# Attention steps written out for all quads, with constant waits, in place of a loop of four steps

## The chip, the cores and the metric

The kernel runs on one core of a Trainium2 chip. The metric is the device time of one execution in microseconds. The engines are TensorE (PE; its weight loads are listed apart as PEld), VectorE (DVE), ScalarE (ACT), GpSimd (POOL) and SyncE (SP, which here only issues DMAs). Each engine runs its own list of instructions in order; the engines meet through semaphores, on which an instruction can wait and which a finished instruction raises.

## The reference

The input x is 16 batches of 512 tokens of 128 channels. One transformer block is computed in f32, cut here to what matters:

```python
h = layernorm(x)
q, k, v = (h @ w_lat @ w_heads for the three)        # 16 heads of 8
att = softmax(causal(q @ k.T / sqrt(8)))
x = x + layernorm((att @ v) @ w_proj + b_proj)
ys = geglu(x @ Ws1 + bs1) @ Ws2 + bs2                # shared feed-forward
top_val, top_idx = top_k((x @ Wr + br) / 1.5, 2)     # 2 of 12 experts
yr = sum over the two of softmax(top_val) * (geglu(x @ We1[e] + be1[e]) @ We2[e] + be2[e])
x = x + layernorm(ys + yr)
```

## The kernel before, in words

Attention comes first, and it is tiled into 64 **quads**: a quad is four heads of one batch, so four quads make a batch. Steps run from `FIRST` = -2 to `LAST` = 65; step g works on three quads at once. It takes the query-major scores of quad g + 2 (`scores_by_query`, `L1229`), from which VectorE reduces the maximum of every row (`L1664`), in five units of two PSUM banks each; it takes the key-major scores of quad g (`scores_by_key`, `L1261`), also in five units, of which ScalarE makes exponentials (`L948`) and GpSimd masks the diagonal blocks (`L721`); and it multiplies the probabilities of quad g - 1 with the values (`products`, `L1308`). Three pairs of PSUM banks are handed round between these units in a fixed order (`EVEN_ITEMS` and `ODD_ITEMS`, `RING` = 3); `wait_emptied` makes TensorE wait until the former unit of a pair of banks has been read.

The row maxima reach the key-major scores by a detour. VectorE joins and negates them (`L1673`), GpSimd splits them into three bf16 parts (`split_maxima`, `L733` to `L739`), TensorE turns them (`turn_maxima`, `L1276`), ScalarE copies them to SBUF (`copy_max_rows`, `L968`), and SyncE moves them by two DMAs per quad into rows of the query matrix (`L555`), so that the subtraction of the maximum is part of the matmul. The first key-major scores of a quad (unit 1) wait for these DMAs (`s_m`, in `scores_by_key`).

Beside that, SyncE stores the parts of later batches' queries and keys (`L510`), loads the queries and keys of quad g + 3 (`load_quad`, `L503`) and, from quad 56 on, writes blank rows (`L536`). Every second step TensorE turns a finished pair of outputs back (`turn_back`, `L1288`), and VectorE normalises it.

The order within a step is written by hand, per engine (`step`, one function per engine). `quad_steps` runs it: steps -2 to 3 are written out, then a hardware loop (`Fori`) of 13 iterations with four steps each covers quads 4 to 55, and steps 56 to 65 are written out again. In the loop the quad's number is a register's value, so that semaphore counts and DMA addresses are computed from it by the engine. Each engine has a loop of its own.

`wait_apart` is a helper for some of the waits: it issues a wait as an instruction by itself, which also raises a semaphore `passed` that nobody waits for. It is used in the attention steps (`L71`), and in the stages behind them: the shared feed-forward, which scatters the rows by expert (`L833`), and the expert tiles of 128 or 256 rows. Of the expert tiles the first 8 and those from 56 on are written out, and 48 run in a loop of eight tiles. In an expert tile VectorE works out the weights (`routed_as`, `L1967` to `L1974`), adds the bias to the finished product (`L2009`) and multiplies with the weight (`L2011`).

The step numbers that a function gets are `gs`, an integer from which buffers are chosen, and `g`, the quad's number, an integer where the step is written out and a register's value in the loop.

Of the kernel before, what the change touches and what calls it, by code (L numbers as in the profile page):

```python
# [13 lines left out]
B, T, C = 16, 512, 128  # L14
# [53 lines left out]
def wait_apart(engine, sem, value, passed):  # L68

    engine.wait_ge(sem, value)  # L70
    engine.sem_inc(passed, 1)  # L71


def ge(engine, sem, value):
# [5 lines left out]
FIRST, LAST = -2, QUADS + 1  # L80
# [13 lines left out]
EARLY = 2  # L94
# [86 lines left out]
def build(nc, a, out):  # L181
    with ExitStack() as ctx:
# [204 lines left out]

            return ROUTE_STEPS * (n - ns % 2) // 2 + ROUTE_STEPS

        def quad_steps(engine, step):  # L390

            for g in range(FIRST, 4):
                step(g, g)
            with engine.Fori(1, B - EARLY) as it:
                for q in range(4):
                    step(4 + q, 4 * it + q)
            for g in range(4 * (B - EARLY), LAST + 1):
                step(g, g)

        LOOPED = PAIRED // 8  # L400
# [37 lines left out]


        GROUPS = tuple(last for _, last in X_LOADS)  # L440

        def rows_of_batch_ready(engine, b):
# [32 lines left out]
        def _(sp):  # L475
# [55 lines left out]
            def step(gs, g):  # L531
# [8 lines left out]
                if 0 <= gs and gs + 3 < QUADS:  # L540

                    if gs > 0:
                        wait_apart(sp, s_st, UNITS * g, s_passed)
                    if gs == 1:
                        sp.wait_ge(s_first_st[1], sum(PARTS))
                    elif gs % 4 == 1:
                        for s in range(2):
                            for n in range(3):
                                wait_apart(sp, s_parts[s][n], SIDE_PARTS[s][n] // 4 * (g - 1), s_passed)
                    load_quad((gs + 3) % 4, g + 3)  # L550
# [7 lines left out]
                if q and projects(gs - gs % 2):  # L558
                    heads_at = 4 * (g - q) + EARLY * HEADS
                    if q == 1:  # L560
                        wait_apart(sp, s_p1, g - q + 2, s_passed)
                        store_late(heads_at, 0, 0)
                    elif q == 2:
                        wait_apart(sp, s_split, 3 * (g - q) + 6, s_passed)
                        store_late(heads_at, 0, 1)
                        store_late(heads_at, 0, 2)
                    else:
                        wait_apart(sp, s_p1, g - q + 4, s_passed)
                        store_late(heads_at, 1, 0)
                elif q == 0 and projects(gs - 4):  # L570
                    wait_apart(sp, s_split, 3 * g, s_passed)
                    store_late(4 * g + (EARLY - 1) * HEADS, 1, 1)
                    store_late(4 * g + (EARLY - 1) * HEADS, 1, 2)

            quad_steps(sp, step)


            sp.wait_ge(s_st, 5 * QUADS)
# [71 lines left out]
        def _(pool):  # L650
# [148 lines left out]
            def step(gs, g):  # L799
# [10 lines left out]
                else:  # L810
# [8 lines left out]
                    mask_unit(gs, g, 3)  # L819
                    split_rows(gs, g, 2)  # L820

            quad_steps(pool, step)


            def scatter(ns, n):
# [37 lines left out]
        def _(act):  # L863
# [141 lines left out]
            def copy_yT(ns, n):  # L1005
# [2 lines left out]
                ge(act, s_proj, n - 1)  # L1008
                act.activation(yT[:, ns % 2, :], ps[:, YT_TURN, :], ACT.Copy).then_inc(s_yTsb, 1)

            quad_steps(act, step)

            act.wait_ge(s_w2, 160)
            act.wait_ge(s_vcur, QUADS)
# [103 lines left out]
        def _(pe):  # L1118
# [306 lines left out]
                                     start=False, stop=(t == NT - 1))  # L1425
                last.then_inc(s_proj, 1)

            quad_steps(pe, step)

            pe.wait_ge(s_exp, UNITS * QUADS)  # L1430
            pe.transpose(ps[:, BE_TURN, 0:6 * E], be_rows[:], ident[0:6 * E, 0:6 * E]).then_inc(s_beT, 1)
# [133 lines left out]
        def _(dve):  # L1565
# [381 lines left out]
                if ns == TABLE_AT:  # L1947
                    tile_table()

            quad_steps(dve, step)  # L1950

            dve.wait_ge(s_vcur, QUADS)
            dve.memset(counted, 0.0).then_inc(s_cset, 1)
# [118 lines left out]
```

## Time and profile before

| | |
|---|---|
| time, median of 3 runs | 1133.36 us (1133.0 to 1135.47) |
| the profiled execution | 1131.17 us |
| its span | 1129.3 us |
| mean granted TensorE clock | 0.953 |
| TensorE matmuls busy | 992.2 us, 8685 instructions |
| VectorE busy | 853.1 us |
| ScalarE busy | 722.5 us |
| GpSimd busy | 632.7 us |

The times in the trace count from the start of the span. Attention's quad 4 starts at 102.45, quad 56 at 486.94; the scatters run from about 590 to 751; the expert tiles end at about 1067, and the last normalisation follows. Engine overlap makes the busy times add up to far more than the span.

### The profile page before, as it was taken

To read this page: it belongs to the slowest core of one execution; us is meant where nothing else is said; L and a number is where in the kernel's file an instruction comes from. 1 tells how busy PE (TensorE), PEld (TensorE's weight loads), DVE (VectorE), ACT (ScalarE), POOL (GpSimd) and SP (SyncE) were. 2 spreads that over 40 slices of the span, in tenths; PEclk is the share of its full clock that TensorE was granted. 3 is DMA by queue.
4 is the path that set the end of the run, shared out by engine and by line. 5 is a ranking of instruction groups with operands and counts; after the bars stand their busy time and mean duration, and the time that the engine had idled before them with its cause. 6 is when DMAs were issued, how large, how long until landed. Compare 5 with 4: busy or idle time off the path is not lost. (4 is left out here: it accounts for less than half of the span.)

```text
span 1129.3 us, 31995 instructions
## 1 busy us (share of the span) xinstructions
PE 992.2 (88%) x8685; PEld 618.6 (55%) x8685; DVE 853.1 (76%) x2487; ACT 722.5 (64%) x1234; POOL 632.7 (56%) x1195
## 2 busy tenths in 40 slices
PE   4589999999999999978879998759999999998774
PEld 2553344443444434433456665339999888897532
DVE  5678888888888888877689985327777777777646
ACT  4578788888888888866646665316565555556426
POOL 4327777777777777755217777742444444444344
PEclk9889999999999999999959998969999999999988
DMA  8413333333333333343251111122222222221176
GB/s 221 104 31 104 112 104 109 113 106 106 105 107 113 113 110 104 107 115 103 74 214 57 54 54 56 51 80 60 61 66 67 60 65 67 63 61 57 32 252 197
DMA packets 135726, 108.21 MB, mean 96 GB/s; under 512 B 32207, under 2 KB 127866, under 8 KB 135658
## 3 DMA queue, kind: packets, MB, share of 16 engines
q1 hardware_dynamic: 124842, 88.19, 27.8%
q0 software_dynamic: 8544, 17.78, 4.4%
q10 hardware_dynamic: 2272, 1.45, 0.5%
q8 instruction: 28, 0.46, 0.2%
q14 instruction: 40, 0.33, 0.1%
HBM read 56.70 MB, written 50.68 MB: 95 GB/s over the span
## 5 line engine op out<-in xcount | busy, mean ns | idle before, releaser
L1664 DVE TENSOR_REDUCE maxima<-ps 128x8 f32<-128x1024 f32 x320 | 380.4, 1222 | 76.7 <-PE ps L1229 69.8
L948 ACT ACTIVATE pT_area<-ps 128x1024 f32<-128x1024 f32 x320 | 320.8, 1023 | 86.2 <-PE ps L1261 80.9
L843 POOL DMA_INDIRECT ys_dram<-quad_area,place_cur x139 | 133.1, 958 | 188.2 <-issue 126.5
L721 POOL TENSOR_SCALAR_AFFINE_SELECT pT_area<-pT_area 128x256 f32<-128x256 f32 (+1 forms) x448 | 186.6, 439 | 90.8 <-ACT pT_area L948 88.3
L1308 PE MATMUL ps<-pT_area,quad_area 128*32 128x512 f32 (+3 forms) x2048 | 185.5, 446 | 0.6 <-POOL pT_area L721 0.6
L833 POOL DMA_INDIRECT xs_dram<-quad_area,idx_cur x128 | 123.1, 961 | 74.6 <-issue 73.7
L1261 PE MATMUL ps<-quad_area 64*128 64x256 bf16 (+3 forms) x1024 | 125.9, 301 | 30.7 <-DMA quad_area<-mT_sb 28.1
L1991 DVE SCALAR_TENSOR_TENSOR quad_area<-ps,be_cur,xnT 128x256 f32<-128x256 f32 (+1 forms) x228 | 92.0, 456 | 61.5 <-PE ps L1541 28.0
L1530 PE MATMUL ps<-quad_area 128*128 128x256 f32 (+1 forms) x456 | 130.3, 368 | 7.0 <-DVE quad_area L1991 6.8
L1096 ACT ACTIVATE xnT<-ps,be_cur 128x256 f32<-128x256 f32 (+1 forms) x228 | 103.1, 453 | 49.2 <-PE ps L1531 48.1
L1229 PE MATMUL ps<-quad_area 61*128 61x128 bf16 (+2 forms) x1792 | 127.0, 241 | 4.7 <-ACT pT_area L948 2.7
L1531 PE MATMUL ps<-quad_area 128*128 128x256 f32 (+1 forms) x456 | 128.0, 362 | 0.0
L1541 PE MATMUL ps<-outT_area,quad_area 128*128 128x128 f32 x834 | 107.8, 278 | 2.7 <-DVE quad_area L2009 2.3
L1541 PEld LDWEIGHTS ps<-outT_area,quad_area 128*128 128x128 f32 x834 | 102.4, 192 | 10.8 <-issue 5.5
L1229 PEld LDWEIGHTS ps<-quad_area 61*128 61x128 bf16 x1792 | 70.1, 94 | 68.8 <-ACT pT_area L948 50.2
L1261 PEld LDWEIGHTS ps<-quad_area 64*128 64x128 bf16 x1024 | 38.4, 94 | 104.9 <-DVE maxima L1664 65.9
L1531 PEld LDWEIGHTS ps<-quad_area 128*128 128x128 f32 x456 | 84.2, 191 | 10.0
L1530 PEld LDWEIGHTS ps<-quad_area 128*128 128x128 f32 x456 | 78.5, 191 | 17.5 <-DVE quad_area L1991 11.0
L1085 ACT ACTIVATE quad_area<-ps 128x256 f32<-128x256 f32 (+1 forms) x76 | 27.7, 365 | 80.3 <-PE ps L1516 80.3
L1308 PEld LDWEIGHTS ps<-pT_area,quad_area 128*32 128x32 f32 x2048 | 43.7, 108 | 57.8 <-issue 48.0
L1081 ACT ACTIVATE quad_area<-pT_area 128x768 f32 x76 | 63.4, 835 | 0.1
L1238 PE MATMUL ps<-mask_of,mask_to 64*128 64x256 bf16 x512 | 50.8, 273 | 5.9 <-DVE maxima L1664 4.8
(234 smaller groups left out, 1501.9 us busy)
## 6 DMA issues: line engine op xcount, KB each, us to landing
qk_dram<-split_area SPq DMA_DIRECT2D x192, 128.0 KB, 2.3
quad_area<-qk_dram SPq DMA_DIRECT2D x256, 96.0 KB, 2.3
row_area<-xs_dram SPq DMA_DIRECT2D x63, 132.0 KB, 2.1
pT_area<-ys_dram SPq DMA_DIRECT2D x16, 512.0 KB, 5.0
pT_area<-in_L_ffn_We SPq DMA_DIRECT2D x12, 384.0 KB, 6.3
out_dram<-pT_area SPq DMA_DIRECT2D x7, 512.0 KB, 3.0
xs_dram<-row_area SPq DMA_DIRECT2D x5, 528.0 KB, 4.4
split_area<-in_L_ffn_We SPq DMA_DIRECT2D x12, 192.0 KB, 3.8
```

What stands on the lines that cost most here:

```text
L721: return pool.affine_select(out=blocks, in_=blocks, compare_op=ALU.is_ge, fill=0.0, base=0, pattern=[[0, count], [1, P]], channel_multipli ...
L833: pool.indirect_dma_start(xs_dram, at, rows_cur[:, b % DEPTH, t, :], None).then_inc(s_scat[par], 16)
L843: pool.indirect_dma_start(ys_dram, at, ys[:, ns % 2, h, :], None).then_inc(s_yst[ns % 2], 16)
L948: act.activation(pT[:, gs % 2, n, :], ps[:, bank:bank + 2, :].rearrange("p a b -> p (a b)"), ACT.Exp).then_inc(s_exp, 1)
L1096: act.activation(gelE[:, ring, 0:width(ns)], ps[:, ring, 0:width(ns)], ACT.Gelu, bias=be_cur[:, ns % 8, 3 + k:4 + k]).then_inc(s_ge, 1)
L1229: return pe.matmul(ps[:, bank + rg, at:at + keys], rows(2 * rg + head, 0, qt * P, qt * P + P, slot, ROWS - 3), rows(2 * rg + head, 1, firs ...
L1261: last = pe.matmul(ps[:, bank + rg, at:at + w], rows(2 * rg + head, 1, kb * P, kb * P + P, slot, ROWS), rows(2 * rg + head, 0, kb * P, T, ...
L1308: last = pe.matmul(ps[32 * i:32 * i + 32, bank, kb * P:T], v_cur[:, slot, kb, i, :], pT[:, buf, n, 512 * rg + at:512 * rg + at + w], start ...
L1530: pe.matmul(ps[:, ring, 0:w], w1_cur[:, par, HR + k * P:HR + (k + 1) * P], xsT[:, par, 0:w], start=True, stop=True)
L1531: pe.matmul(ps[:, ring, RT:RT + w], w1_cur[:, par, k * P:(k + 1) * P], xsT[:, par, 0:w], start=True, stop=True).then_inc(s_he, 1)
L1541: last = pe.matmul(ps[:, Y_BANKS[par], h * C:(h + 1) * C], hidT[:, par, k, h * P:(h + 1) * P], w2_cur[:, par, k * C:(k + 1) * C], start=(k ...
L1664: dve.tensor_reduce(to, ps[:, bank:bank + 2, :].rearrange("p a (j k) -> p a j k", k=P), AX, ALU.max).then_inc(s_mxf, 1)
```

## The change

`quad_steps` writes out all steps, from `FIRST` to `LAST`, on all five engines, with integers throughout, and no longer needs the engine. `wait_apart` issues the instruction that raises `passed` only where the value is not an integer. With a constant value only the wait is left, and a wait that stands alone is carried by the next instruction of the engine. The second edit holds for every use of `wait_apart` in the kernel, also behind attention.

```diff
 def wait_apart(engine, sem, value, passed):
 
     engine.wait_ge(sem, value)
-    engine.sem_inc(passed, 1)
+    if not isinstance(value, int):
+        engine.sem_inc(passed, 1)
...
-        def quad_steps(engine, step):
-
-            for g in range(FIRST, 4):
-                step(g, g)
-            with engine.Fori(1, B - EARLY) as it:
-                for q in range(4):
-                    step(4 + q, 4 * it + q)
-            for g in range(4 * (B - EARLY), LAST + 1):
+        def quad_steps(step):
+
+            for g in range(FIRST, LAST + 1):
                 step(g, g)
...
-            quad_steps(sp, step)
+            quad_steps(step)
...
-            quad_steps(pool, step)
+            quad_steps(step)
...
-            quad_steps(act, step)
+            quad_steps(step)
...
-            quad_steps(pe, step)
+            quad_steps(step)
...
-            quad_steps(dve, step)
+            quad_steps(step)
```

## Rows read from the trace of the kernel before

**Rows 1.** The page's first part: busy time, share of the span, instructions, by engine.

```profile
PE 992.2 (88%) x8685; PEld 618.6 (55%) x8685; DVE 853.1 (76%) x2487; ACT 722.5 (64%) x1234; POOL 632.7 (56%) x1195
```

**Rows 2.** Table by stretch: length, busy time by engine, granted clock, DMA share, GB/s.

```profile
core 0: us, PE busy (x) PEld busy (x) DVE busy (x) ACT busy (x) POOL busy (x), PEclk, DMA share, GB/s
...
309.69:339.25 29.56, 27.98 (x355) 11.91 (x352) 25.73 (x32) 23.92 (x30) 21.35 (x55) 1.00 0.38 108
...
102.45:486.94 384.49, 363.81 (x4579) 154.87 (x4576) 334.38 (x391) 310.93 (x391) 277.29 (x703) 1.00 0.38 108
...
486.94:546.60 59.66, 47.74 (x587) 20.61 (x588) 40.64 (x56) 38.56 (x47) 30.31 (x92) 0.94 0.35 94
```

**Rows 3.** Waits of TensorE, 102.45 to 486.94: total us, times, longest.

```profile
PE ps L1261 <- DMA quad_area<-mT_sb: 20.1, 26, 1.2
```

**Rows 4.** Timeline, a looped pair's start, us, instruction, [idle before].

```profile
309.16 0.39 PE L1261 MATMUL ps<-quad_area 64*128 64x384 bf16 x4 [0.62 <-DMA quad_area<-mT_sb]
...
309.69 1.02 ACT L948 ACTIVATE pT_area<-ps 128x1024 f32<-128x1024 f32 x1 [0.67 <-PE ps L1261]
...
318.00 5.77 DVE L1664 TENSOR_REDUCE maxima<-ps 128x8 f32<-128x1024 f32 x5
...
319.29 0.39 PE L1261 MATMUL ps<-quad_area 64*128 64x256 bf16 x4
319.36 0.22 POOL L739 TENSOR_TENSOR m_part<-m_rest,m_part 128x16 bf16<-128x16 f32 x1 [0.18 <-POOL m_part L737]
...
320.72 0.26 ACT L968 ACTIVATE mT_sb<-ps 48x128 bf16<-48x128 bf16 x1
...
321.20 1.61 SPq L555 DMA_DIRECT2D quad_area<-mT_sb  x2
...
324.13 0.40 PE L1261 MATMUL ps<-quad_area 64*128 64x384 bf16 x4 [0.89 <-DMA quad_area<-mT_sb]
```

**Rows 5.** Timeline, the second pair of the same looped pass.

```profile
334.13 0.39 PE L1261 MATMUL ps<-quad_area 64*128 64x256 bf16 x4
...
335.56 0.26 ACT L968 ACTIVATE mT_sb<-ps 48x128 bf16<-48x128 bf16 x1
...
338.72 0.39 PE L1261 MATMUL ps<-quad_area 64*128 64x384 bf16 x4 [0.64 <-DMA quad_area<-mT_sb]
```

**Rows 6.** Timeline, quads 2 and 3, written out ahead of the loop.

```profile
87.53 0.39 PE L1261 MATMUL ps<-quad_area 64*128 64x384 bf16 x4 [1.17 <-DVE maxima L1664]
...
87.96 1.02 ACT L948 ACTIVATE pT_area<-ps 128x1024 f32<-128x1024 f32 x1 [0.53 <-PE ps L1261]
...
97.44 0.39 PE L1261 MATMUL ps<-quad_area 64*128 64x256 bf16 x4
...
98.80 0.26 ACT L968 ACTIVATE mT_sb<-ps 48x128 bf16<-48x128 bf16 x1
...
99.08 1.60 SPq L555 DMA_DIRECT2D quad_area<-mT_sb  x2
...
101.92 0.39 PE L1261 MATMUL ps<-quad_area 64*128 64x384 bf16 x4 [0.63 <-DMA quad_area<-mT_sb]
```

**Rows 7.** Timeline of SyncE's DMA issues: stores written out, stores looped.

```profile
92.32 1.88 SPq L510 DMA_DIRECT2D qk_dram<-split_area  x3
...
315.13 2.19 SPq L510 DMA_DIRECT2D qk_dram<-split_area  x3
```

**Rows 8.** Lines, 1035 to 1068: busy us, mean ns | idle before.

```profile
L2009 DVE TENSOR_TENSOR quad_area<-ps,quad_area 128x128 f32<-128x128 f32 x12 | 3.4, 284 | 0.0
L2011 DVE TENSOR_TENSOR quad_area<-quad_area,weight_cur 128x128 f32<-128x128 f32 x11 | 3.2, 292 | 1.6
L1971 DVE SCALAR_TENSOR_TENSOR weight_other<-row_area,be_cur 128x1 f32<-128x1 f32 x10 | 2.1, 213 | 0.0
L1974 DVE TENSOR_TENSOR weight_cur<-weight_cur,weight_other 128x1 f32<-128x1 f32 x10 | 1.6, 159 | 1.5
```

**Rows 9.** Lines of GpSimd, 590 to 760: the scatters.

```profile
L833 POOL DMA_INDIRECT xs_dram<-quad_area,idx_cur x127 | 121.8, 959 | 40.3 <-issue 39.4 <-ACT quad_area L1031 0.6 <-DVE idx_cur L1919 0.3
```

**Rows 10.** DMA queues, 140 to 490, then 73 to 140: packets, MB, share.

```profile
q1 hardware_dynamic: 44169, 37.81, 37.7%
...
q8 instruction: 6, 0.10, 0.7%
```

## The prediction

> **What bounds the kernel now.** I read the page's first part, then the table by stretch, then the waits of the looped stretch, and then the timelines of one looped pass beside a pair of steps that is already written out. On the page TensorE is the busiest engine, 88% of the span [rows 1]. The table shows where the change can act most: the looped steps, quads 4 to 55, take 384.49 of the 1129.3 us, at the full granted clock, 1.00, with TensorE busy 363.81 us; one pass of four quads takes 29.56 us [rows 2]. So TensorE idles some 20.7 us there, and nearly all of that is one wait: 20.1 us in 26 waits, one per pair of quads, before the first key-major scores of an even step, for the transposed maxima that come back by DMA [rows 3].
>
> A pair of steps is a ring through that wait. The maxima's rows land; TensorE runs back to back through the even step and most of the odd one to the matmul group of unit 4 (the row of width 256); ScalarE copies the turned maxima (`L968`); SyncE issues two DMAs (`L555`); they land, and the next even step starts. Every delay in this ring lengthens the kernel; a delay beside it doesn't. In the looped pass the reader is to follow four points per pair [rows 4, 5]:
> - first pair: start 309.16, unit 4 at 319.29, end of the copy 320.72 + 0.26 = 320.98, next start 324.13. Parts 10.13, 1.69 and 3.15 us, together 14.97.
> - second pair: start 324.13, unit 4 at 334.13, end of the copy 335.82, next start 338.72. Parts 10.00, 1.69, 2.90, together 14.59.
> - the pair written out ahead of the loop: start 87.53, unit 4 at 97.44, end of the copy 99.06, next start 101.92 [rows 6]. Parts 9.91, 1.62, 2.86, together 14.39.
>
> All three end in the same wait for the DMA, and do the same work, so the difference is what the loop costs. Two places show where it comes from. An exponential that follows the scores starts 0.14 us after their end in the loop (309.55 to 309.69) and 0.04 after it where its wait is a constant (87.92 to 87.96) [rows 4, 6]: a wait on a computed count has register work ahead of it. And SyncE, whose every address and count is computed in the loop, takes 2.19 us for three stores against 1.88 [rows 7], so that in the first pair it comes to the maxima's DMAs at 321.20, 0.22 after the copy's end, against 0.02 in the written-out one [rows 4, 6].
>
> **The change, part by part.** The sum is made on the profiled execution, 1131.17 us, of which 1129.3 are the span; it is 2.19 us under the median of the runs, 1133.36.
>
> 1. *The loop goes, on all five engines.* 13 passes are 26 pairs. At the written-out pair's 14.39 us they take 374.1 instead of 384.49: **-10.4 us**. By parts and pass that is 0.22 + 0.07 + 0.29 in the first pair and 0.09 + 0.07 + 0.04 in the second, 0.78 us, 13 times, and 0.2 because the passes' mean is 29.58. Ends: if only SyncE's lateness and the loop's seam go, all pairs become like the second, 14.59: -5.1. The best case is set by what is late next. VectorE's five reductions run without a gap from 318.00 to 323.77 [rows 4], 0.36 before TensorE's start at 324.13, and the ring of PSUM banks hangs on them; so a pair can shrink from 14.59 to about 14.23 before VectorE ends it: -14.5. I take the written-out pair, because it is the same code as the one that will run.
>
> 2. *The separate wait goes where its value is a constant* (`wait_apart`: the count `passed` is no longer raised, so the wait rides on the next instruction). The written-out pair still holds these, so what they cost comes on top. By the code TensorE has nine per pair: two ahead of the first query-major scores (`s_qk`), four ahead of the masked units, two ahead of the turned maxima, one ahead of the projection. The dearest price that the trace has for such a wait is 0.15 us of idle time, on VectorE [rows 8]; nine of those would be 1.35 us, more than the ring can give, since VectorE ends it at 14.23: so 0 to 0.16 us per pair, 0 to 4.2 in 26. I go near the low end, 0.04 per pair, **-1.0 us**: TensorE's matmuls run without a gap past most of these places in both stretches, so the queue is ahead of them and the 0.39 us of a matmul group cover the wait; only where TensorE has just been idle is nothing queued ahead. GpSimd's four per step, with which it splits the maxima, end at 319.58, before the matmuls of unit 4 that come ahead of the turn are through (319.68) [rows 4], and SyncE's stand ahead of its loads and stores, beside the ring. No wait is added to any engine.
>
> 3. *Quads 56 to 63* (59.66 us [rows 2]) were written out before; only the waits of point 2 change, in four pairs: **-0.3**, at most 4 x 0.16 = 0.6 by the same cap.
>
> 4. *The shared stage and the scatter.* GpSimd's scatters set the pace, 127 x 0.959 us of busy time and 40.3 of issue [rows 9]; their waits aren't of this kind. Of their idle time 0.9 us is put down to other engines, which the change can speed up: a third of it, **-0.3**, between 0 and 0.9.
>
> 5. *The last routed tiles, which are written out.* VectorE has two such waits per tile, before the product with the weight (`L2011`: 1.6 us idle over 11) and before the sum of the weights (`L1974`: 1.5 over 10) [rows 8]; the instructions ahead of them (`L2009`, `L1971`) have none. 0.15 + 0.15 us per tile, taken at 0.25 because a wait on the instruction isn't free, for ten tiles: **-2.5**. Zero if TensorE or the transfer of the weights paces these tiles, -3.5 at most. The 6 x 8 tiles that stay in their loop keep registers and keep the separate waits.
>
> 6. *More instructions to bring in.* In the loop only queue 1 moves packets; in 73 to 140 us, straight code up to about 100 and then the loop's first pass, six blocks of 16 KB come through queue 8 and take 0.7% of 16 engines over 67 us, so 67 x 16 x 0.007 / 6 = 1.25 us each [rows 10]. Those 67 us hold some four pairs of new code, 1.5 blocks each, so the 24 pairs that now become new code will need some 36 more. Priced **0**: the written-out pair of 14.39 us lies inside that stretch and TensorE runs back to back in it. If the cover fails, 36 x 1.25 = 45 us.
>
> Sum: 10.4 + 1.0 + 0.3 + 0.3 + 2.5 = **14.5 us**, so 1116.7 in an execution like the profiled one, and 1133.36 - 14.5 = **1119** against the median.
>
> The Trainium skill, "Runtime: NRT & Kernel Launch", section "Instruction fetch mechanics", says two things that bear on points 1 and 6. Straight code is streamed ahead block by block and crossing a block is mostly hidden, which is what rows 10 show beside a pair of 14.39 us; but a taken branch whose target is out of the window forces a fetch before the engine can go on. Read flatly, each of the 13 passes would now pay a fetch that the change saves, 13 x 1.25 = 16 us, an estimate with the trace's own duration for a block, and the gain would be about 26 us in place of 14.5. The trace doesn't bear that out, as the third rival works out.
>
> **The rivals.**
> - *Only the seam and SyncE's lateness go; the ring stays at the second pair's 14.59.* For it: the 0.20 us between 14.59 and 14.39 might come from the early quads, where less is in flight (that pair issues its loads at another time). Against it: it is spread over all three parts, as register work would be. A gain of 5.1 + 4.1 = 9.2 us, or of 6.7 if the last tiles don't follow: 1124 to 1127.
> - *VectorE's reductions become the bound at 14.23, because the separate waits are worth 0.16 and more.* 26 x 14.23 = 370.0, 3.1 us below the 373.1 of points 1 and 2, and up to 2 more in points 3 to 5: 1113 to 1116. For it: the margin is only 0.36 us, so the ring is near it anyway. Against: nothing in the trace shows a pair below 14.39.
> - *The branch back costs a fetch of code.* 1133.36 - 16 - 10.4 = about 1107. Against it: no packet of an instruction queue in 140 to 490 us [rows 10], and the pair with the seam is longer than the other by only 0.38 us, which is in point 1 already; a fetch of 1.25 us has no room in it.
> - *Nothing changes.* The loop's register work could lie in time that the ring waits anyway, and the written-out pair be short for want of stores from two quads earlier: 1133. Against it: it issues three stores and four loads like the others.
> - *Slower: TensorE's straight code isn't brought in in time.* Its place is the even step and the odd one, where TensorE is busy 14.0 us of a pair (363.81 / 26) [rows 2]: a block that comes late stalls it in the ring itself. 36 blocks; from 14.5 / 36 = 0.40 us per block on, the gain is gone, and with the whole 1.25 the time is 1133 - 14.5 + 45 = 1164. For it: five engines would fetch at once, beside transfers that take 38% of the DMA engines [rows 2]. Against it: rows 10 beside rows 6, where blocks arrive and the pair is the shortest of the three.
>
> **How the numbers follow.** Forecast 0.60 (1116 to 1123: point 5 at its ends, point 2 from 0 on, and a pair between 14.3 and 14.5); first rival 0.18; VectorE's bound 0.08; branch 0.03; nothing 0.05; slower 0.06. A measurement of this kernel can tell 0.2%, 2.3 us, from no change. Faster: 0.60 + 0.18 + 0.08 + 0.03 less a hundredth for the first rival's weakest end, 0.88; same 0.06; slower 0.06. The range goes from 1113, where most of the VectorE case is in, to 1127, which takes in the first rival: it leaves out some 0.05 below and 0.12 above.
>
> **What would show it.** Point 1: starts of even steps (`L1261` at width 384, the first of a step) 14.3 to 14.4 us apart and all alike, with no difference between odd and even pairs; exponentials 0.04 us after the scores; three stores in 1.88 us. Point 2: no idle time put down to issue before `L1238` and `L1276`. Point 5: no idle time before `L2011` and `L1974`, and a shorter stretch between the last looped tile and the end. Point 6: some 36 more packets of 16 KB on queue 8, and TensorE's idle time before matmuls not grown. The prediction is wrong if pairs stay at 14.6 and the wait before `L1261` merely has another releaser (VectorE's `L1664`), or if gaps of 0.4 us or more open on TensorE where blocks of code arrive.

## The result, and the profile after

The changed kernel takes 1114.19 us in the median of 4 runs (1112.48 to 1115.93), the kernel before 1134.34 in 4 runs beside it: a ratio of 0.983, 95% interval 0.981 to 0.9849. Once more on another occasion it was 1115.16 (6 runs) against 1133.97 (14 runs), 0.9833 (0.9803 to 0.9864). It is faster by 17 to 22 us; the forecast was 1119, range 1113 to 1127.

The two profiled executions differ by less, 1129.3 - 1112.3 = 17.0 us of span. Most of it lies in the quads that were looped. The page's first part after the change, for TensorE, and the table by stretch (length, busy time by engine, granted clock, DMA share, GB/s) for quads 2 and 3, quads 4 to 55, and the 59.6 us behind them:

```profile
PE 978.1 (88%) x8685; PEld 616.1 (55%) x8685; DVE 849.8 (76%) x2487; ACT 722.9 (65%) x1234; POOL 633.2 (57%) x1195
```

```profile
87.32:101.65 14.33, 13.62 (x180) 5.96 (x176) 12.49 (x14) 12.00 (x15) 10.60 (x28) 1.00 0.41 114
101.65:474.40 372.75, 354.06 (x4580) 154.68 (x4576) 330.65 (x391) 311.95 (x390) 276.60 (x703) 1.00 0.41 114
474.40:534.00 59.60, 48.03 (x588) 20.54 (x588) 41.02 (x57) 38.70 (x47) 30.82 (x92) 0.94 0.35 93
```

Quads 4 to 55 take 372.75 us where they took 384.49 [rows 2]: 11.74 us, the pairs of steps now all alike at 14.32 to 14.37. One pair, in the timeline that answers to [rows 4 to 6] (line numbers move from kernel to kernel: `L1257` here is `L1261` of the kernel before):

```profile
301.95 0.40 PE L1257 MATMUL ps<-quad_area 64*128 64x384 bf16 x4 [0.70 <-DVE maxima L1660]
...
302.38 1.02 ACT L944 ACTIVATE pT_area<-ps 128x1024 f32<-128x1024 f32 x1 [0.65 <-PE ps L1257]
...
310.48 5.74 DVE L1660 TENSOR_REDUCE maxima<-ps 128x8 f32<-128x1024 f32 x5
...
311.75 0.39 PE L1257 MATMUL ps<-quad_area 64*128 64x256 bf16 x4
...
313.11 0.26 ACT L964 ACTIVATE mT_sb<-ps 48x128 bf16<-48x128 bf16 x1
...
313.39 1.56 SPq L551 DMA_DIRECT2D quad_area<-mT_sb  x2
...
316.27 0.39 PE L1257 MATMUL ps<-quad_area 64*128 64x384 bf16 x4 [0.69 <-DVE maxima L1660]
```

The parts of the ring are 9.80 (301.95 to 311.75), 1.62 (to 313.37) and 2.90 us (to 316.27). The exponential starts 0.03 us after the scores' end (302.35 to 302.38), SyncE comes to the maxima's DMAs 0.02 us after the copy. What is new is the releaser: in TensorE's waits from 101.65 to 474.40 VectorE stands where the DMA stood [rows 3]:

```profile
PE ps L1257 <- DVE maxima L1660: 18.3, 26, 0.7
```

The second piece lies in the last routed tiles. From the same tile (56) to the last one, before and after, by the table by stretch of each kernel, and VectorE's lines after (1020 to 1051), which answer to [rows 8]:

```profile
999.12:1066.30 67.18, 58.77 (x405) 52.41 (x404) 50.07 (x212) 40.44 (x93) 28.16 (x30) 1.00 0.18 50
```

```profile
987.48:1050.51 63.03, 58.20 (x406) 52.28 (x404) 50.40 (x211) 39.75 (x93) 28.45 (x30) 1.00 0.19 53
```

```profile
L2007 DVE TENSOR_TENSOR quad_area<-quad_area,weight_cur 128x128 f32<-128x128 f32 x10 | 2.9, 291 | 0.3
...
L1970 DVE TENSOR_TENSOR weight_cur<-weight_cur,weight_other 128x1 f32<-128x1 f32 x10 | 1.6, 159 | 0.3
```

The idle time ahead of the two VectorE instructions falls from 0.15 to 0.03 us each, the period of a single-half tile from 3.17 to 2.93, and the stretch by 4.15 us. Quads 0 to 3 give another 0.44 (29.42 to 28.98 between exponentials). Together 16.3 us; the other stages shift by up to 1.6 us, either way.

More code is fetched, as forecast: 62 blocks of 16 KB on queue 8 against 28, 34 more. Queue 8 is taken here for TensorE's code, because it moves 28 blocks in every kernel below that keeps TensorE's loop, whatever the other engines do, and 62 or more in every one that writes TensorE's steps out.

Not every separate wait became part of an instruction. Of TensorE's eight per pair (208 in the quads that were looped, 0.051 us each) four are left (104). By the code those are the four that stand beside another wait, ahead of the first query-major scores and of the turn; the four ahead of the masked units, which stand alone, are gone.

### The profile page after: what moved, and what is told of

Same layout as the page of the kernel before. It is cut to its first block, busy times and chain, and to the rows that moved or that the text cites. A ratio compares the mean times of both kernels' runs of the same rounds, so it can differ in the third digit from the quotient of the medians.

```text
span 1112.3 us, 28174 instructions
## 1 busy us (share of the span) xinstructions
PE 978.1 (88%) x8685; PEld 616.1 (55%) x8685; DVE 849.8 (76%) x2487; ACT 722.9 (65%) x1234; POOL 633.2 (57%) x1195
## 4 chain that ended last, share of the span: by engine, by line
PE 20%; POOL 9%; DMA 7%; issue 6%; DVE 5%; DVEq 2%; ACT 1%; ACTq 1%; SPq 0%; POOLq 0%
POOL xs_dram L829 9%; PE ps L1526 5%; PE ps L1527 5%; PE ps L1537 5%; DMA ys_dram<-quad_area,place_cur 5%; DVEq L1981 1%; DMA xs_dram<-quad_area,idx_cur 1%; DVE quad_area L1987 1%; PE ps L1512 1%; DMA out_dram<-pT_area 1%; PE ps L1552 1%; PE ps L1555 0%; DVE place_cur L1963 0%; ACT pT_area L1109 0%; PE ps L1420 0%
## 5 line engine op out<-in xcount | busy, mean ns | idle before, releaser
L1257 PE MATMUL ps<-quad_area 64*128 64x256 bf16 (+3 forms) x1024 | 124.9, 301 | 28.8 <-DVE maxima L1660 21.4
L1225 PEld LDWEIGHTS ps<-quad_area 61*128 61x128 bf16 x1792 | 66.3, 95 | 69.1 <-ACT pT_area L944 50.3
L1257 PEld LDWEIGHTS ps<-quad_area 64*128 64x128 bf16 x1024 | 37.6, 94 | 104.3 <-DVE maxima L1660 85.1
L1527 PEld LDWEIGHTS ps<-quad_area 128*128 128x128 f32 x456 | 84.5, 192 | 10.1
```

Source lines behind the costliest of these rows:

```text
L1225: return pe.matmul(ps[:, bank + rg, at:at + keys], rows(2 * rg + head, 0, qt * P, qt * P + P, slot, ROWS - 3), rows(2 * rg + head, 1, firs ...
L1257: last = pe.matmul(ps[:, bank + rg, at:at + w], rows(2 * rg + head, 1, kb * P, kb * P + P, slot, ROWS), rows(2 * rg + head, 0, kb * P, T, ...
L1527: pe.matmul(ps[:, ring, RT:RT + w], w1_cur[:, par, k * P:(k + 1) * P], xsT[:, par, 0:w], start=True, stop=True).then_inc(s_he, 1)
```

## The experiments

Each edit alone, the changed kernel again and the kernel with the expert tiles written out were timed beside the kernel before (1133.97 us, 14 runs). The others ran once each, and of those only the stretches of the trace are used.

**The second edit alone.** All engines keep their loop:

```diff
-            quad_steps(step)
+            looped_steps(sp, step)      # the loop of four of before; so for pool, act, pe, dve
```

> Only the second edit: the loop of four steps stays on all engines, and waits with constant values lose their separate instruction. My theory (the gain is two independent pieces, the loop and the separate waits of the last routed tiles): pairs of quads in the loop stay at 14.97 and 14.59 us and end in the wait for the maxima's DMA, quads 4 to 55 take 384 to 385 us, the last single-half tiles go from 3.17 to 2.93 us, and the whole is 4 to 5 us under the kernel before. Rival (the separate waits hold up the written-out quads and the shared stage too, and the loop is the smaller piece): 7 us or more under it.

1127.32 us (7 runs), ratio 0.9935 (0.9912 to 0.9958). In the trace quads 4 to 55 take 384.28 us with pairs of 14.95 and 14.60; the stretch of the last tiles is what it is in the changed kernel (63.27 by the same two tiles). So the waits give about 4 us at the end and, as long as the loop is there, nothing in it. By the medians it is 6.7 (interval 4.8 to 10.0), between the two theories; the pieces in the traces come to 4.1 and speak for the first. The traced execution of the kernel before was itself 2.8 us under the median of its 14 runs (1131.17 against 1133.97), about the difference between 4.1 and 6.7; no other trace of that kernel is there to say in which stage.

**The first edit alone.** All quads written out, every separate wait kept:

```diff
-    if not isinstance(value, int):
-        engine.sem_inc(passed, 1)
+    engine.sem_inc(passed, 1)
```

> Only the first edit: all quads written out, every such wait stays an instruction of its own that raises the count. My theory as predicted: pairs at 14.39 us, as the pair that was written out before, with the maxima's DMA ending the wait before the first key-major scores; quads 4 to 55 374 us; last tiles at 3.17; 10.5 to 12 us under the kernel before. Rival (the pair is at VectorE's reductions as soon as the loop is gone, and the separate waits are worth nothing): pairs at 14.33 with VectorE as releaser, 372.7 us. Second rival (the separate waits were what the pair lost): pairs at 14.55 or more, under 7 us gained.

1127.03 us (8 runs, 1117.85 to 1131.07), ratio 0.9943 (0.9919 to 0.9966). Quads 4 to 55, and the ring in the same place as above:

```profile
100.23:475.74 375.51, 357.67 (x4580) 155.21 (x4576) 330.54 (x391) 311.70 (x390) 276.89 (x702) 1.00 0.40 113
```

```profile
302.13 0.39 PE L1256 MATMUL ps<-quad_area 64*128 64x384 bf16 x4 [0.68 <-DVE maxima L1659]
...
312.04 0.39 PE L1256 MATMUL ps<-quad_area 64*128 64x256 bf16 x4
...
313.39 0.26 ACT L963 ACTIVATE mT_sb<-ps 48x128 bf16<-48x128 bf16 x1
...
313.68 1.56 SPq L550 DMA_DIRECT2D quad_area<-mT_sb  x2
...
316.55 0.39 PE L1256 MATMUL ps<-quad_area 64*128 64x384 bf16 x4 [0.66 <-DVE maxima L1659]
```

Pairs of 14.43 us: the loop is worth 384.49 - 375.51 = 9.0 us and the separate waits 375.51 - 372.75 = 2.8. In this pair all of the waits' 0.1 us lies in the first part, 9.91 against 9.80; the other parts are the same, 1.61 and 2.90. Beside the timeline of the changed kernel TensorE falls back by 0.05 and 0.04 us at the two masked units of the even step, whose separate waits are the ones that went. Neither theory nor rival had the number. The last tiles stay at 3.18 us.

This kernel was traced a second time, because its first traced execution was by far the shortest of its eight runs.

> The kernel with all quads written out and every separate wait kept, a second time: its profiled execution was the shortest of eight, 1117.85 us against a median of 1127. If the other executions are longer in attention (SyncE's issues held up by blocks of code, as where SyncE alone is looped), quads 4 to 55 come out over 377 us with pairs that stray from 14.43; if in the stages behind it or ahead of it, at 375 to 376 us, and the difference stands in the granted clock of those stages.

```profile
102.49:477.90 375.41, 357.73 (x4579) 155.33 (x4576) 330.55 (x391) 311.72 (x391) 276.89 (x702) 1.00 0.40 113
477.90:546.11 68.21, 57.48 (x636) 23.59 (x633) 43.83 (x73) 43.72 (x53) 32.91 (x97) 0.87 0.30 82
```

```profile
475.74:539.64 63.90, 53.40 (x637) 22.78 (x633) 44.02 (x73) 43.39 (x52) 32.86 (x97) 0.95 0.32 87
```

The quads that were looped agree within 0.1 us. The span is 11.1 us longer all the same: 2.2 ahead of quad 4, 4.3 in quads 56 to 63, where the granted clock is 0.87 here and 0.95 (second fence) there, 2.2 up to the first routed tile and 1.8 in the next eight, which ran at 0.96 and 1.00. So whole executions of one kernel scatter by several us in stages that the change hardly touches, while the stretch it aims at repeats. That is why the pieces are taken from the traces. The medians of the two edits do not add up either: 6.7 and 6.9 us make 13.6 of 18.8, where the pieces in the traces, 4.1, 9.0 and the 2.6 that the waits give only without the loop, make 15.7. That this scatter makes the difference is not shown.

**The changed kernel again, and with the expert tiles written out too.**

> The changed kernel itself once more, as the comparison for the other three on this chip. By the traces, which differ by 17.0 us of span, 17 to 18 us under the kernel before; by the medians first measured, 20. The stages differ between the profiles by 12.7 us up to the last exponential, by 4.2 in the last tiles, and by some 1 us more where the granted clock rises later or earlier; if the last is chance, it scatters between executions and the difference of medians comes out between 16 and 20.

1115.16 us, 18.8 less than before; quads 4 to 55 take 372.65.

```diff
-            for n in range(8):
-                step(n, n)
-            with engine.Fori(1, LOOPED) as it:
-                for k in range(8):
-                    step(8 + k, 8 * it + k)
-            for n in range(8 * LOOPED, ROUTED + 2):
+            for n in range(ROUTED + 2):
                 step(n, n)
```

> The changed kernel with the loop of the 48 expert tiles written out as well. My theory (TensorE is busy through these tiles, 100.80 of 101.00 us in the looped stretch, so there is nothing for waits and registers to cost): written-out full tiles took 4.15 us against 4.19 to 4.20 looped, so 2 to 2.5 us less than the changed kernel at best, 0 to 2.5 in all. Rival (the gain of 0.24 us per tile at the end holds for all tiles): 48 x 0.24 = 11.5 us less.

1110.35 us (5 runs, 1108.48 to 1114.65), ratio to before 0.9796 (0.9767 to 0.9825). From tile 8 to the last, first the changed kernel, then this one:

```profile
784.42:1050.51 266.09, 261.06 (x1669) 235.89 (x1668) 199.94 (x739) 157.50 (x335) 120.42 (x126) 1.00 0.22 62
```

```profile
785.94:1050.64 264.70, 259.73 (x1671) 238.85 (x1669) 203.08 (x739) 157.92 (x336) 120.86 (x126) 1.00 0.23 63
```

1.4 us: the first theory. It is the fastest of all versions by its median, 4.8 us under the changed kernel, but the runs of the two overlap (1109.84 to 1118.83 there) and the trace shows only the 1.4 as its own.

**Does VectorE now set the pair?** The releaser's name said so. In the kernel before, VectorE's run of reductions already ended near the next start: 0.36 us ahead of it at the end of the pair of 14.97 [rows 4], but only 0.10 at the end of the pair of 14.59 (338.62 against 338.72 [rows 5]):

```profile
332.85 5.77 DVE L1664 TENSOR_REDUCE maxima<-ps 128x8 f32<-128x1024 f32 x5
```

To separate the two, half of one reduction is left out:

```diff
+                if gs % 2 and u == 0 and 4 <= gs < 56:
+                    dve.tensor_reduce(grid[:, 0:1, 0, 0:16:5], ps[:, bank:bank + 1, :].rearrange("p a (j k) -> p a j k", k=P), AX,
+                                      ALU.max).then_inc(s_mxf, 1)
+                    return
```

> The changed kernel with half of one reduction left out: in the odd steps of quads 4 to 55 unit 0 is reduced over one PSUM bank instead of two, so the maxima of one row group there are old ones. It takes some 0.6 us of work from VectorE per pair. My theory (after the change VectorE's run of reductions ends each pair, and the maxima's DMA lands only 0.1 us before it): a pair shrinks by about 0.1, to 14.2 to 14.25, and the wait before the first key-major scores has the DMA as releaser again; quads 4 to 55 369 to 370.5 us. Rival (VectorE alone sets the pair, with nothing close behind): 14.33 - 0.6 = 13.7, 357 us. Second rival (neither; TensorE's own work sets it): 14.33, 372.7.

```profile
99.20:471.82 372.62, 354.06 (x4580) 154.67 (x4576) 321.16 (x392) 311.94 (x390) 276.77 (x703) 1.00 0.40 114
```

```profile
PE ps L1257 <- DMA quad_area<-mT_sb: 18.1, 26, 0.7
```

```profile
325.50 2.36 DVE L1664 TENSOR_REDUCE maxima<-ps 128x8 f32<-128x1024 f32 x2 [0.28 <-PE ps L1225]
...
328.08 0.40 PE L1257 MATMUL ps<-quad_area 64*128 64x384 bf16 x4 [0.70 <-DMA quad_area<-mT_sb]
```

VectorE's busy time falls by 9.5 us, the stretch by 0.1, and the DMA is the releaser again. VectorE's last reduction now ends 0.22 us ahead of the start (327.86 to 328.08) where it ended 0.05 ahead (316.22 to 316.27); more the cut does not give, because the reductions behind it wait for TensorE's scores. My theory falls: there was no 0.1 us to win behind VectorE. Its reductions and the landing of the maxima came within a tenth of a microsecond of each other, VectorE last by a hair, and the ring through the DMA sets the pair as before. The other side of the same question, six raises of the unused count ahead of the maxima's DMAs:

```diff
                     sp.wait_ge(s_mT, g + 2)
+                    if gs % 2 and 4 <= gs < 56:
+                        for _ in range(6):
+                            sp.sem_inc(s_passed, 1)
```

> The changed kernel with six raises of the unused count ahead of the maxima's two DMAs in the odd steps of quads 4 to 55, between their wait and their issue, so that SyncE issues them d later (some 0.3 us; the trace will say). My theory (0.1 us of room between the landing and VectorE's end): each pair grows by d - 0.1, to about 14.5, quads 4 to 55 to 377 or 378, and the releaser is the DMA again. Rival (the ring through the DMA still sets the pair): by d in full, 14.6, 380.5. Second rival (the DMA has lost its hold for good): 14.33 as before.

```profile
101.55:484.46 382.91, 354.02 (x4579) 154.64 (x4576) 332.81 (x392) 311.94 (x390) 277.03 (x704) 1.00 0.39 111
```

```profile
318.47 0.26 ACT L967 ACTIVATE mT_sb<-ps 48x128 bf16<-48x128 bf16 x1
...
319.15 1.58 SPq L554 DMA_DIRECT2D quad_area<-mT_sb  x2
```

SyncE now issues 0.42 us after the copy's end (318.73), 0.39 later than without the raises; pairs are 14.73, longer by 0.40. The delay counts in full: the rival, and what the prediction had said of the ring.

**Which engine's loop costs what.** One or several engines keep the loop of four (`looped_steps`), the others are written out; the second edit is in all of them. First SyncE alone written out:

> Only SyncE's steps are written out; the other four engines keep the loop of four. The second edit is in. My theory (SyncE's lateness at its seam and in its stores makes the first pair of a pass longer, everything else is spread over the registers of the other engines): all pairs alike at 14.55 to 14.6, quads 4 to 55 379 to 379.5 us, 5 less than with all looped. Rival (SyncE's part is the whole loss): 14.33 to 14.4, 373 to 375. Second rival (SyncE has nothing to do with it): 14.97 and 14.59 as before.

```profile
100.53:480.98 380.45, 363.74 (x4579) 154.88 (x4576) 333.62 (x391) 310.92 (x390) 277.25 (x703) 1.00 0.38 109
```

Pairs of 14.72 and 14.54: SyncE's loop was worth 384.28 - 380.45 = 3.8 us, not 5, and a difference between first and second pair remains that belongs to the other engines' seam. Then TensorE or ScalarE alone looped:

> TensorE alone keeps the loop of four, so its waits hold register values and stay separate; the other four are written out. Theory (TensorE's register work and its separate waits lie in the ring, between the landing of the maxima and unit 4 of the odd step, and are most of the 0.30 us per pair by which the kernel with SyncE alone written out lies over 14.33): pairs 14.45 to 14.6, quads 4 to 55 376 to 379 us, almost no 16 KB blocks. Rival (ScalarE's and VectorE's register waits are the larger part): 14.33 to 14.4, 373 to 374.5.

> ScalarE alone keeps the loop of four. The prediction put part of the loop's price on exponentials that start 0.10 us later after the scores. Theory (these and the later copy of the maxima lie in the ring): pairs 14.40 to 14.50, quads 4 to 55 374.5 to 377 us. Rival (only the copy lies in it): 14.33 to 14.40, under 374.5.

```profile
101.66:478.53 376.87, 360.16 (x4580) 154.26 (x4576) 331.52 (x391) 311.96 (x391) 277.96 (x703) 1.00 0.39 111
```

```profile
101.36:477.93 376.57, 357.65 (x4578) 153.67 (x4576) 332.32 (x392) 310.68 (x390) 277.20 (x703) 1.00 0.40 112
```

4.1 us for TensorE and 3.8 for ScalarE over 372.7, first and second pairs of 14.52 and 14.47, and of 14.53 and 14.44: both theories hold, and each of the two takes about a third of what the loop and its waits cost together. ScalarE has none of the separate waits in its code, so its 3.8 us are the loop's alone; its exponentials start 0.13 us after the scores again (304.06 to 304.19):

```profile
303.66 0.40 PE L1267 MATMUL ps<-quad_area 64*128 64x384 bf16 x4 [0.71 <-DMA quad_area<-mT_sb]
304.19 1.02 ACT L954 ACTIVATE pT_area<-ps 128x1024 f32<-128x1024 f32 x1 [0.76 <-PE ps L1267]
```

VectorE and GpSimd alone were not tried.

SyncE alone looped came out against every theory:

> The other way round: SyncE alone keeps the loop of four, all other engines are written out. My theory: SyncE comes late to the maxima's DMAs by some 0.2 to 0.3 us once in four steps, of which 0.1 is covered; pairs 14.5 and 14.33 in turn, quads 4 to 55 374 to 375.5 us. Rival (the parts don't add, SyncE's lateness was only the other engines' registers handed on): 372.7. Second rival (SyncE's part is the whole loss): 384.

```profile
100.93:494.44 393.51, 356.27 (x4579) 154.72 (x4576) 333.46 (x392) 311.98 (x391) 277.10 (x703) 1.00 0.38 107
```

9 us *more* than with everything looped, pairs from 14.37 to 17.36. The timeline shows SyncE taking 3.18 us for four loads where it takes 1.86 to 2.0, and coming to the maxima's DMAs 1.92 us after the copy (321.91). The DMA queues from 320 to 323.5 show a block of code:

```profile
320.60 3.18 SPq L509 DMA_DIRECT2D quad_area<-qk_dram  x4
...
321.65 0.26 ACT L974 ACTIVATE mT_sb<-ps 48x128 bf16<-48x128 bf16 x1
...
323.83 0.80 SPq L561 DMA_DIRECT2D quad_area<-mT_sb  x1
```

```profile
q8 instruction: 1, 0.02, 2.6%
```

In this trace 13 single DMA issues of SyncE take over 1 us (normal are 0.3 to 0.8), and each one coincides with a block on queue 8. The changed kernel has nine of them in quads 4 to 55, all on a block, as this one (SyncE's timeline, then the queues from 302.57 to 305.48):

```profile
302.57 2.87 SPq L499 DMA_DIRECT2D quad_area<-qk_dram  x4
```

```profile
q1 hardware_dynamic: 503, 0.45, 56.8%
q8 instruction: 1, 0.02, 2.0%
```

There it costs nothing. So one more run, without TensorE's blocks:

> TensorE and SyncE keep the loop of four, ScalarE, VectorE and GpSimd are written out. It answers why the kernel with SyncE alone in a loop came out slower than the kernel before (393.5 us for quads 4 to 55, pairs of 14.4 to 17.4). Theory F (blocks of TensorE's code, fetched only where its steps are written out, hold up a DMA issue of SyncE by 1 to 1.7 us, and SyncE in a loop has no slack for that): without those blocks no issue over 1.1 us after the first pass, regular pairs, first of a pass 14.8 to 15.0 and second 14.4 to 14.6, quads 4 to 55 380 to 384 us. Rival (SyncE in a loop can't keep up with engines that are written out, fetch or no fetch): irregular pairs again, over 387 us.

```profile
101.76:485.18 383.42, 360.15 (x4580) 154.24 (x4576) 332.36 (x392) 311.96 (x390) 278.09 (x703) 1.00 0.38 109
```

```profile
q1 hardware_dynamic: 45279, 38.71, 38.0%
q14 instruction: 17, 0.14, 0.1%
q8 instruction: 1, 0.02, 0.0%
```

(The second fence lists the queues from 112 to 470 us.) One block instead of 33, no issue over 1 us, regular pairs of 14.96 and 14.52, 10.1 us less with one engine *more* in the loop. The rival falls, and the blocks are the cause. But theory F names only part of the way. With SyncE alone looped, four of the long pairs (15.92, 15.68, 15.37 and 15.84 us) hold no issue over 0.85 us. There SyncE waits 1.3 to 1.7 us for its own stores to land before it may load, and each time a block on queue 8 falls into the stores' flight; in the kernel without the blocks no such wait is over 0.7. One of the four, SyncE's timeline and its waits from 252 to 262 us:

```profile
255.12 2.19 SPq L516 DMA_DIRECT2D qk_dram<-split_area  x3
260.31 1.87 SPq L509 DMA_DIRECT2D quad_area<-qk_dram  x4
```

```profile
SPq L72 <- DMA qk_dram<-split_area: 2.1, 2, 1.7
```

Every pair over 15 us in that trace has a held issue or such a wait; these four make up about 3.2 us over the 14.9 of an undisturbed first pair.

## Why the prediction was right

- **The bound.** The ring through the maxima's DMA was read rightly and still holds after the change: delaying its DMAs by 0.39 us costs 0.40 per pair, and letting VectorE end 0.17 earlier gives nothing. The prediction counted a new releaser at unchanged pairs of 14.6 as a sign that it is wrong; the new releaser came, at 14.33, and meant nothing. By time and releaser alone, 1114 to 1115 us would fit the second rival (VectorE's bound, 1113 to 1116) as well; the pairs, 14.33 and not 14.23, and these two runs speak against it.
- **Point 1, the loop:** forecast -10.4 us, measured -9.0. The written-out pair of [rows 6] was taken as steady, 14.39; the same code runs at 14.43 over 26 pairs, and the 0.04 us lie in the last part, 2.90 against 2.86. The causes named, registers ahead of waits and SyncE's lateness at the seam, are both there: 3.8 us for SyncE's loop with the others looped, 3.8 and 4.1 for ScalarE's and TensorE's with the others written out (TensorE's with its separate waits). That the branch back costs a fetch is not borne out: with TensorE alone looped, the pair with the seam is longer than the other by 0.05 us. (That rival's 1107 also leaves out points 2 to 5; with them it would be 1103.)
- **Point 2, the separate waits in those quads:** -1.0, measured -2.8. The argument that a matmul group covers TensorE's waits was too strong: the first part of the ring shrinks by 0.11 us. The count was off too: eight per pair and not nine, since the wait for the projection is one of the four ahead of masked units, and only four of them went. The cap on this term, 4.2 from VectorE's margin, held, but for no good reason: it takes the margin of the longer pair, 0.36, off the length of the shorter one, where the margin was 0.10, and VectorE's run moves along with the ring. That `L1276` would lose its idle time put down to issue was wrong: its weight load still waits 0.41 us per turn. Before `L1238`, 19.8 us in 65 waits put down to issue became 10.7 in 26, now put down to VectorE.
- **Point 3, quads 56 to 63, and point 4:** -0.3 each, not to be told. One kernel's two executions differ by 4.3 us in those quads. Point 2's own price, 0.04 a pair, would have given 0.2 for point 3. That the scatters have no such wait was wrong by the code, which has one ahead of each batch's eight; without its raise their idle time is 40.2 us against 40.3 [rows 9].
- **Point 5, the last tiles:** -2.5, measured -4.15. That is beyond the -3.5 given as the most. The price per tile was near, 0.25 against 4.15 / 19 = 0.22; the count was not. I took the ten tiles of the window that I had read, but all tiles from 56 on are written out, 19 periods in the stretch that shortened.
- **Point 6, the blocks of code:** 36 forecast, 34 came, priced 0, and 0 it was. But the place at which they can cost, which the last rival put on TensorE, is SyncE. Nine of its issues over 1 us in quads 4 to 55 fall on blocks in the changed kernel too; there SyncE has time to spare: it comes to the maxima's DMAs at most 0.6 us after the copy, and only in even steps, whose maxima land some 0.9 us before they are wanted. That cover is what the price of 0 rests on, and the prediction had not named it. It is thin: with the first edit alone, one block among the stores made SyncE wait 2.2 us for their landing, and that pair took 14.67 us in place of 14.43. The Trainium skill, "Runtime: NRT & Kernel Launch", section "Instruction fetch mechanics", calls the crossing of a block mostly hidden. For TensorE itself the traces agree: pairs with one block and pairs with two take the same 14.32 to 14.37 us. The cost that these runs show falls on another engine's DMAs.

The terms measured sum to 11.74 + 4.15 + 0.44 = 16.3 us against 14.5. That they came so near is partly luck: point 1 was 1.4 us too high, points 2 and 5 were 1.8 and 1.65 too low. The medians give 18.8 with an interval of 15.4 to 22.3; the first comparison, 17.1 to 21.6, lies just above 16.3. Of the 2.5 us between 16.3 and 18.8, 1.8 stand between the traced executions and the medians: the kernel before was traced 2.8 us under its median, the changed one 1.0 under its own (1114.12 against 1115.16). In which stage the usual executions of the kernel before spend that time is open.

## What to carry to other kernels

A loop over registers costs little per instruction, but where a ring of engines waits for one another each tenth of a microsecond counts on every lap: compare one looped lap with a written-out one in the same trace, part by part, and count how often the lap repeats. A releaser is only who came last; delay one arrival and relieve the other before believing that the bound has moved. Writing out TensorE's steps sent its code through the DMA engines, and the engine that issues DMAs needed slack for that: here it paid to write that engine out first (3.8 us gained) and cost 9 us to leave it for last.

## What the runs showed of the hardware

A block of TensorE's code that arrives while SyncE issues a DMA can hold that issue up by 0.6 to 1.7 us. It is no price per block: in quads 4 to 55 of the changed kernel 9 of 36 blocks do it to over 1 us. A block that arrives while stores are in flight can also delay their landing: SyncE's longest wait for it was 1.7 us with SyncE alone looped, and 0.7 with TensorE looped too, where the blocks were missing. With SyncE looped and all others written out the two came to at least 393.51 - 383.42 = 10.1 us over 52 quads (the second kernel has TensorE's loop to pay as well) and ate more than the whole gain there.

Where a wait had stood alone ahead of an instruction, taking out its separate raise made it vanish as an instruction; where two waits stood together, one stayed (208 against 104 on TensorE).
